# Row maxima on 32-row blocks in alternating pairs, a norm moved to ScalarE, and a new order

## The reference, cut to what matters

```
q, k, v = split(x @ w_qkv)                  # 16 heads of 8
scores = where(causal, q @ k.T / sqrt(8), min)
attn = softmax(scores)                      # needs the row maxima for range
o = (attn @ v) @ w_o
h = layernorm(x + o, g1, b1)                # the norm ahead of the router
probs = softmax(h @ wg)                     # top 2 of 8
```

## Time and profile before

| | us |
|---|---|
| median of 3 runs (lowest, highest) | 1057.57 (1057.13, 1059.99) |
| the profiled execution, its own time | 1060.96 |
| span of that execution, first to last instruction | 1059.2 |
| TensorE matmuls busy | 907.8 (86%) |
| TensorE weight loads busy | 724.8 (68%) |
| VectorE busy | 827.8 (78%) |
| ScalarE busy | 729.2 (69%) |
| GpSimd busy | 590.5 (56%) |

### The profile page before, as it was taken

The page is one execution under the profiler, slowest core; times in us unless marked ns, Lnnn a source line. Parts: engine busy times, 40 slices in busy tenths (PEclk is TensorE's granted clock), DMA queues, the critical chain, the costliest instruction groups (busy, mean ns, idle before and its releaser), DMA issues. The chain is left out here.

```text
span 1059.2 us, 26980 instructions
## 1 busy us (share of the span) xinstructions
PE 907.8 (86%) x7519; PEld 724.8 (68%) x7519; DVE 827.8 (78%) x2292; ACT 729.2 (69%) x1795; POOL 590.5 (56%) x781
## 2 busy tenths in 40 slices
PE   2469999999999999999999988840999999999474
PEld 1347777776776777766777666520999999999421
DVE  2459899899899999988989777665677777766378
ACT  4766898888888878878876554530766776666356
POOL 8001344446666666767677666874466666665400
PEclk9568999999999999999999989965999999999788
DMA  1045454435445445435443544052333333332196
GB/s 55 13 107 136 108 124 117 112 89 134 120 120 130 104 116 137 130 94 134 119 115 103 148 113 132 23 131 80 98 98 98 94 87 97 97 90 63 39 254 191
DMA packets 138080, 115.22 MB, mean 109 GB/s; under 512 B 18400, under 2 KB 126564, under 8 KB 137968
## 3 DMA queue, kind: packets, MB, share of 16 engines
q1 hardware_dynamic: 120880, 92.76, 34.5%
q0 software_dynamic: 8640, 16.93, 5.0%
q10 hardware_dynamic: 8448, 4.20, 1.4%
HBM read 61.12 MB, written 52.58 MB: 107 GB/s over the span
## 5 line engine op out<-in xcount | busy, mean ns | idle before, releaser
L577 POOL TENSOR_SCALAR_AFFINE_SELECT b_PT<-b_PT 128x256 f32<-128x256 f32 (+1 forms) x384 | 193.6, 518 | 202.2 <-ACT b_PT L763 198.3
L1074 DVE TENSOR_REDUCE b_m_neg<-b_ps_m 128x2 f32<-128x512 f32 (+1 forms) x384 | 256.1, 680 | 56.8 <-PE b_ps_m L1476 35.2
L763 ACT ACTIVATE b_PT<-b_ps_s 128x512 f32<-128x512 f32 x384 | 223.7, 599 | 63.6 <-PE b_ps_s L1455 35.3
L1798 POOL DMA_INDIRECT results<-e_Y,e_X x142 | 161.8, 1139 | 106.4 <-issue 68.3
L1826 ACT ACTIVATE e_h<-e_ps,e_w 128x256 f32<-128x256 f32 x284 | 111.8, 475 | 77.1 <-PE e_ps L1899 71.3
L612 POOL DMA_INDIRECT slots<-c_pay,b_pos x128 | 128.7, 1006 | 43.2 <-issue 31.1
L1906 PE MATMUL e_ps_y<-e_w,e_h 128*128 128x128 f32 x1136 | 140.4, 277 | 3.0 <-ACT e_h L1826 3.0
L1906 PEld LDWEIGHTS e_ps_y<-e_w,e_h 128*128 128x128 f32 x1136 | 134.4, 194 | 3.3 <-ACT e_h L1826 3.3
L1476 PE MATMUL b_ps_m<-c_QK 128*128 128x256 f32 x512 | 121.0, 325 | 0.0
L1455 PE MATMUL b_ps_s<-c_QK 128*128 128x512 f32 x256 | 118.3, 471 | 2.5 <-ACT b_PT L763 2.1
L1469 PE MATMUL b_ps_m<-c_QK 128*128 128x128 f32 x512 | 96.7, 312 | 0.0
(11 more groups left out here) (217 smaller groups left out, 2188.1 us busy)
## 6 DMA issues: line engine op xcount, KB each, us to landing
c_QK<-qk_scr SPq DMA_DIRECT2D x128, 192.0 KB
qk_scr<-b_qk_hi SPq DMA_DIRECT2D x64, 256.0 KB
e_X<-slots SPq DMA_DIRECT2D x71, 130.0 KB
qk_scr<-b_qk_lo SPq DMA_DIRECT2D x32, 256.0 KB
f_G<-results SPq DMA_DIRECT2D x32, 256.0 KB, 3.6
a_X<-in_L_attn_x_dram SPq DMA_DIRECT2D x16, 256.0 KB
x<-a_X SPq DMA_DIRECT2D x16, 256.0 KB
b_X<-x SPq DMA_DIRECT2D x32, 128.0 KB
```

What stands on the lines that cost most here:

```text
L577: nc.gpsimd.affine_select(out=tri, in_=tri, compare_op=ALU.is_ge, fill=0.0, base=0, pattern=[[0, tri.shape[1]], [1, P]], channel_multiplie ...
L763: nc.scalar.activation(PT[:, g % 2, q % 3], ps_s[:, q % 2], ACT.Exp, scale=HD ** -0.5).then_inc(s_e, 1)
L1074: nc.vector.tensor_reduce(out, scores, AX.X, ALU.max, negate=True).then_inc(s_red, 1)
L1798: nc.gpsimd.indirect_dma_start(dram["results"][:, :], bass.IndirectOffsetOnAxis(X[:, j.of(NB_X), u, D:D + 1].bitcast(u32), 0), Y[:, n, u, ...
```

## The change

Four things are changed.

First, the maxima. A unit is now one head block j and all of its groups (units 0 to 3) or two of them (units 4 to 11), and its products use only the 24 rows of that block, in both operands. Units come in pairs on two different row blocks and two PSUM buffers: both masks first, then the products of the two units alternately. A pair waits until both units of the pair before have been reduced.

```
-            def maximum(b, u):
+            def maxima(b, pair):
                 if not b.exists(B):
                     return
-                n = b.of(NQ)
-                if u == 0:
+                n, units = b.of(NQ), (2 * pair, 2 * pair + 1)
+                if pair == 0:
                     need(pe, s_qkr[n], b.turn(NQ) * READS + READS)
-                need(pe, s_red, 12 * b + (u - 1))
...
+                need(pe, s_red, 12 * b + 2 * pair)
+                for u in units:
+                    if u < 4:
+                        nc.tensor.matmul(ps_m[:, u % 2].rearrange("p (g k) -> p g k", g=NG), ident_b[:, :], mask_b[:, :, :],
+                                         start=True, stop=False, skip_group_check=True)
...
+                last = NG if pair < 2 else 2
+                for i in range(last):
+                    for u in units:
+                        j, g = unit(u)
+                        at = slice(32 * j, 32 * j + ROWS)
+                        if u < 4:
+                            done = nc.tensor.matmul(ps_m[:, u % 2, i * P:(i + 1) * P], QK[at, n, j, i, 0:P], QK[at, n, NJ, i, 0:P],
+                                                    start=False, stop=(i == last - 1), skip_group_check=True)
+                        else:
+                            done = nc.tensor.matmul(ps_m[:, u % 2, i * T:(i + 1) * T], QK[at, n, j, g + i, P:T], QK[at, n, NJ, g + i, :],
+                                                    start=False, stop=(i == last - 1), skip_group_check=True)
+                        if i == last - 1:
+                            done.then_inc(s_b, 1)
```

```
                 if (s - 1).exists(B):
+                    b, n = s - 1, (s - 1).of(NQ)
+                    need(sync, s_qkw[n], b.turn(NQ) * WRITES + WRITES)
                     need(sync, s_s, (b - NQ) * 12 + 12)
                     if b.base < NQ:
                         sync.wait_ge(s_fill, FILLED - 2 * (NQ - 1 - n))
-                    sync.dma_start(QK[M_ROW:M_ROW + 1, n, 0:NJ].rearrange("o j g n -> o (j g) n").bitcast(fp32), zero_row[:, :]).then_inc(s_qkr[n], 16)
```

Third, `hidden_norm` goes to ScalarE, with a shift from VectorE:

```
+            def hidden_norm(q):
+                need(act, s_sh1, q + 1)
+                need(act, s_h1, q)
+                for t in range(2):
+                    last = nc.scalar.activation(H0[:, t, :], R[:, t, :], ACT.Identity, bias=shift1[:, t:t + 1], scale=rstd1[:, t:t + 1])
+                last.then_inc(s_h0, 1)
...
+            def hidden_shift(q):
+                need(dve, s_rstd1, q + 1)
+                need(dve, s_h0, q)
+                nc.vector.scalar_tensor_tensor(out=shift1[:, :], in0=mv1[:, :, 0], scalar=-1.0, in1=rstd1[:, :],
+                                               op0=ALU.mult, op1=ALU.mult).then_inc(s_sh1, 1)
```

More of the change, by code:

```diff
@@ L256, in layers @@
         rstd1 = sb("b_rstd1", [P, 2])
+        shift1 = sb("b_shift1", [P, 2])
         H0 = sb("b_H0", [P, 2, D])
@@ L385, in layers @@
         s_rstd1 = sem("b_rstd1s")
+        s_sh1 = sem("b_sh1")
         s_h0 = sem("b_h0")
@@ L497, in step @@
                         sync.wait_ge(s_fill, FILLED - 2 * (NQ - 1 - n))
-                    sync.dma_start(QK[M_ROW:M_ROW + 1, n, 0:NJ].rearrange("o j g n -> o (j g) n").bitcast(fp32), zero_row[:, :]).then_inc(s_qkr[n], 16)
-                if (s - 1).exists(B):
-                    b, n = s - 1, (s - 1).of(NQ)
-                    need(sync, s_qkw[n], b.turn(NQ) * WRITES + WRITES)
                     rows = scr[n].rearrange("(a s) (r j g) n -> j (s r) a (g n)", a=2, g=NG, j=NJ)
@@ L631, in step @@
                     cell_divisor(gi)
+                    mask(c, 1)
                     sends(s, 1)
-                    mask(c, 1)
                     mask(c, 2)
@@ L864, in step @@
                     exp(c, 0)
+                    root_out(q)
                     evac_o(p)
                     exp(c, 1)
-                    rows_high(a)
                     cell_rms(gj)
                     exp(c, 2)
-                    root_out(q)
+                    rows_high(a)
                     exp(c, 3)
                     exp(c, 4)
+                    hidden(r)
+                    exp(c, 5)
                     columns_high(a)
-                    exp(c, 5)
-                    hidden(r)
+                    hidden_norm(q)
+                    maxima_row(b1)
+                    exp(c, 6)
+                    route_gap(routed)
                     cell_input(gh)
-                    maxima_row(b1)
-                    route_gap(routed)
-                    exp(c, 6)
-                    exp(c, 7)
-                    cell_root(ge)
-                    root_in(n)
                     logits(r)
                     attended(p)
+                    exp(c, 7)
+                    route_ranks(routed)
                     exp(c, 8)
-                    route_ranks(routed)
                     exp(c, 9)
+                    cell_root(ge)
                     exp(c, 10)
                     exp(c, 11)
+                    root_in(n)
                     values_in(a)
@@ L892, in step @@
                     exp(c, 0)
+                    cell_rows(gf)
                     exp(c, 1)
-                    cell_rows(gf)
                     root_out(q)
+                    exp(c, 2)
                     evac_o(p)
-                    exp(c, 2)
+                    exp(c, 3)
+                    exp(c, 4)
                     rows_high(a)
-                    exp(c, 3)
                     cell_high(gf)
-                    exp(c, 4)
+                    exp(c, 5)
                     columns_high(a)
-                    exp(c, 5)
                     cell_inverse(gi)
+                    hidden_norm(q)
                     hidden(r)
                     exp(c, 6)
-                    maxima_row(b1)
                     exp(c, 7)
                     exp(c, 8)
+                    maxima_row(b1)
+                    cell_softplus(gf)
+                    attended(p)
                     logits(r)
-                    attended(p)
-                    cell_softplus(gf)
                     route_ranks(routed)
+                    cell_squares(gi)
                     exp(c, 9)
@@ L1212, in hidden_norm @@
                 need(dve, s_rstd1, q + 1)
-                need(dve, s_h1, q)
-                for t in range(2):
-                    last = nc.vector.tensor_scalar(H0[:, t, :], R[:, t, :], mv1[:, t, 0:1],
-                                                   rstd1[:, t:t + 1], ALU.subtract, ALU.mult)
-                last.then_inc(s_h0, 1)
+                need(dve, s_h0, q)
+                nc.vector.scalar_tensor_tensor(out=shift1[:, :], in0=mv1[:, :, 0], scalar=-1.0, in1=rstd1[:, :],
+                                               op0=ALU.mult, op1=ALU.mult).then_inc(s_sh1, 1)
             def columns_low(a):
@@ new lines, in maxima @@
+                need(pe, s_red, 12 * b + 2 * pair)
[4 more added lines that the diff above has]
+                    else:
+                        nc.tensor.matmul(ps_m[:, u % 2].rearrange("p (g k) -> p g k", g=2)[:, :, P:T], ident_b[:, :], mask_b[:, 0:2, :],
+                                         start=True, stop=False, skip_group_check=True)
```

174 lines of the change are left out of this document (74 added, 100 removed).

## The result

The change makes the kernel slower: 1124.74 us median (1116.53 to 1128.47, 4 runs) against 1058.67 (1057.13 to 1059.99, 4 runs of the kernel before on the same chip). The ratio is 1.0614, 95% interval 1.0546 to 1.0682. The forecast was 1041, the range ended at 1071. The profiled execution took 1128.47 us (span 1126.7), so it is 3.7 over the median, as before it was 3.4 over.

What follows compares the result with a forecast made beforehand. TensorE was taken to bound 8 double steps and VectorE the 8 with routing; gains of 8 and 8.8 us sum to 16.8, bringing the median from 1057.57 to 1041 us, range 1020 to 1071.

Steps and rivals of the forecast that it cites:

- What bounds before: Steady stage: TensorE sets the double steps without routing (36.15 us), VectorE those with routing (41.06 us), 8 of each.
- The row blocks: Maxima on TensorE: loads of two blocks go side by side, 0.11 us for two, saving 1.5 us per double step.
- rival (a): Loads of two row blocks do not go side by side, TensorE wins nothing: 1080 us, chance 0.22.
- The change of form: TensorE entering and leaving row-block products: 0.19 us per pair, six pairs a step, 1.14 us; ends 0 and 0.20.
- The lock-step: A pair on TensorE waits for both reductions of the last pair: costs 0.3 us per double step, ends 0 and 1.3.
- The ring of 14.0 us: Six rounds of TensorE's pair and VectorE's two reductions fit a step of about 17.5 us, so the wait does not bind.
- The norm: Moved to ScalarE: VectorE saves 1.1 us per double step, ScalarE gains 1.5; cost taken 0.2 in TensorE-bound double steps.
- near 39: Sign that the forecast is right: length in us of double steps with routing, 41.06 before.
- The small terms: Zeroing transfer, GpSimd fill at the start, norms exposed after 670 us: transfer and late norms taken as 0, fill hidden.
- zeroing transfer: Leaving it out of the transfer queue gains 0, since its issue is hidden; ends 0 and 16 us.
- the two waits of 0.3: TensorE waits about 0.3 us at pairs 4 and 0 in the new even order, not at all in the odd.
- rival (b): The lock-step and ScalarE take the gain back, 1.3 + 0.4 against 1.5 us per double step: 1058 us, chance 0.14.

Runs made afterwards that it cites:

- e1: Kernel before with only the router's norm moved to ScalarE, in the old order: 1052.65 us, ratio 0.9925.
- e8: Changed kernel (new order, norm on ScalarE, joint wait) with 128-row products in place of 24-row ones, zeroing transfer kept: 1096.41 us, ratio 1.0326.
- e7: Changed kernel without row blocks and joint wait: new order, norm on ScalarE, old 128-row units with own waits: 1079.56 us, ratio 1.0180.
- e5: Kernel before with the joint wait alone, the two 128-row units of a pair moved together, old order: 1110.27 us, ratio 1.0451.
- e12: Kernel before with a second zeroing transfer per step behind the first on the same queue: 1059.72 us, ratio 1.0009.
- e4: Kernel before with the new order of all four engines alone, own 128-row units and waits, norm on VectorE: 1085.56 us, ratio 1.0224.
- e2: Kernel before with the 24-row pairs and their joint wait, norm on VectorE, old order: 1154.27 us, ratio 1.0873.
- e6: Kernel before with 24-row products alone, units at old places with own waits, no alternation or zeroing transfer: 1198.64 us (two runs).

## Why the prediction was wrong

**What bounds before**: right, and e1 confirms it; TensorE's double step did not gain by a lighter VectorE, the routed one did.

**The row blocks**: loads and products of two blocks go side by side, as predicted; rival (a) is wrong in its mechanism, and that the kernel became slower, as it said, is luck. The change of form was mis-sized: taken as 0.19 per pair from products on column blocks, it is 1.13 - 0.43 - 0.44 = 0.26 in the first kind and 0.76 - 0.21 - 0.22 = 0.33 in the second. A double step then wins 4 x 0.11 - 8 x 0.04 = 0.1 us in place of 1.5. This takes 8 x 1.4 = 11 us out of the sum; it is no loss by itself.

**The lock-step** is the first failed step: "it does not bind by itself", +0.3 (ends 0 and 1.3) per double step. By e8 less e7 it is 17 us, 1.1 for each of 16 double steps, near the upper end; by e5, in the old order and with the move of the units, 49 us, 3.1 each, far over it. The ring of 14.0 us in a step of 17.5 adds up TensorE's and VectorE's times without walking VectorE's order. The wait at 346 us comes from what stands between two reductions there: I had found 0.3 us ahead of pairs 4 and 0 of the even step, and the 2.14 us stand ahead of its pair 3, which waits for reductions 4 and 5 of the odd step, behind the scan.

**The norm**: right. By the totals of the two profiles VectorE's busy time falls from 827.8 us to 806.1 in e1 and ScalarE's rises from 729.2 to 750.9. Over 16 double steps that is -1.4 and +1.4 each, where -1.1 and +1.5 were predicted; the routed double step went to 38.96 ("near 39"), the other lost 0.20 (predicted 0.2). The sum of that part, -8.8 + 8 x 0.2 = -7.2, stands against 0.9925 x 1061 - 1061 = -8.0.

**The small terms**: zeroing transfer 0, confirmed by e12. The start was counted at nothing and costs 5 us by the new order.

**The new order** had no term of its own beyond the two waits of 0.3 found for TensorE; alone it costs 24 us (e4), 5.8 at the start and 17.3 in the steady part. This is the second failed step: the walk through TensorE's order stood for the orders of all engines, and which waits it missed stays open.

**The clock** had no term at all, and this is the third failed step and the largest omission. The earlier trace rows show 1.00 before, and I took it as given. With 24-row products nearly the same idle time brings 0.94: 28 us from e8 to the change in the new order, 44 from e5 to e2 in the old one. The full-speed work that is missing grows by 31 and 43 us, as much as that, with pairs that cost TensorE no more per step than the old units at full clock. The Trainium skill, "TensorE: Matmul & The Clock Gate", Part 1, A second HAM failure mode: psum-queue depth-cycling, tells of a kernel whose short idle times between groups of matmuls let the clock go back and forth between its levels; the trace after the change agrees in kind (346 to 362 us). That the stretches at the lower level become more or longer with 24-row products, or come without a gap (e6), is shown by the runs alone. From 64 to 24 rows the changes of form are equally many, so there the fall goes with the rows; from 128 to 64 the rows and the change of form are not apart. Why fewer rows bring the clock down is not shown.

**The parts together**, as steps of the ratio in the new order: order 2.2%, norm -0.4, joint wait 1.5, row blocks 2.9; together 6.1. The steps depend on what is there already: in the old order joint wait (with the move) and row blocks are 4.5 and 4.2. The 66 us lie outside the forecast's range and beyond every rival; rival (b) adds up to 1059 us, not 1058, which changes nothing.

Kernel e1 beats both kernels: 1052.65 us, and the only part of the change that is worth keeping is the norm on ScalarE.

## What to carry to other kernels

A new order is a part of a change with a price of its own: walk every engine's order, not TensorE's alone, and separate it from the rest by a run with the order only. Before small blocks of rows replace whole-array products, ask whether TensorE has gaps nearby, because here nearly equal gaps cost 28 us more with 24 rows than with 128; and one pair must contain enough products to earn back some 0.3 us for the change of form. If a wait shrinks and the time grows, look for what that wait covered.

## What was not expected of the hardware

- The granted clock fell to its lower level in a stretch in which TensorE was recorded busy without a gap (e6, 138 to 146 us in the windows shown, then 0.59), and at an idle time of 33 to 35 us of 480 it averaged 0.99, 0.96 and 0.94 with products of 128, 64 and 24 rows (over whole runs, by the medians, 0.93, 0.92 and 0.90).
- After a standstill of 2.14 us TensorE ran some 13 us at half its clock, though it had work all the time; after one of 2.59 us in e8, with products of 128 rows, the clock stayed up (after another it fell for a shorter time).
- A change from whole-array products to a row block and back costs 0.28 to 0.29 us around one unit and 0.26 to 0.33 around a pair; it does not depend on whether the block has 24 or 64 rows (1.13 and 1.12 us for a pair).
